# Inner pairs of four duos in one unit with x standing, in place of two half-empty units

## The chip, the cores and the metric

The kernel runs on one NeuronCore of a Trainium2 chip. The metric is the device time of one execution in microseconds. Before the change the median of three runs is 1236.45 us (1236.43 to 1236.52).

## The reference

The kernel computes a small recommendation model over a batch of 2048 samples, all in fp32. Each of 40 fields looks up a row of 64 numbers in its own table. For every pair of fields i < j (780 pairs), each with its own 64x64 matrix W, one number is computed: the row of i times W, dotted with the row of j. The 780 numbers and 16 dense inputs of a sample go through three layers.

```python
e = jnp.stack([tbl_0[ids[:, 0]], ..., tbl_39[ids[:, 39]]], axis=1)      # 2048 x 40 x 64
viW = jnp.einsum('bpd,pde->bpe', e[:, i_idx, :], W)                      # 780 pairs
z = jnp.einsum('bpe,bpe->bp', viW, e[:, j_idx, :])
h = jnp.concatenate([z, dense_ctx], axis=1)                              # 796 wide
h = jnp.maximum(h @ W_top1 + b_top1, 0.0)                                # 796 x 512
h = jnp.maximum(h @ W_top2 + b_top2, 0.0)                                # 512 x 256
y = h @ W_top3                                                           # 256 x 1
```

## The kernel before, in words

**Tiles.** The batch is cut into NB = 4 blocks of 512 samples, each of four subs of 128. Two fields form a duo (20 per block), four duos a quad (5 per block). GpSimd gathers a duo's table rows with samples on partitions into `rows` (12 slots, one per duo). TensorE turns a duo with four transposes (`duo`, L908) into PSUM, and ScalarE copies it to `x` (24 slots), where one field's 64 numbers lie on partitions 0 to 63 and the other's on 64 to 127, and 512 samples lie along the columns. For duos 0 to 3 of block 0 nothing is gathered: their rows are looked up by matmuls of small tables, held in SBUF, with tables of zeros and ones that VectorE builds (L1051, `hot`); the result is x directly, and `rows` never holds them.

**Units.** A unit fills two PSUM banks with 128 x 1024 numbers (x times W), and VectorE multiplies them with the other field's numbers in one instruction. There are three kinds:
- F (L940): W stands (it is the operand loaded into the array), x of duo n moves. Two matmuls of 64 x 128 by 512 columns, one in the upper and one in the lower 64 rows of the array. Its result has the numbers of a pair on partitions and samples along columns. It covers four pairs between two duos.
- D: the same instructions for the pairs inside a duo, of two duos at once. Each half of the array computes one pair only, so half of the result's 128 rows belong to no pair. There is one D unit for two duos, 10 per block, counted among the 120 standing units of a block.
- R (L936): x stands, W moves; its result has samples on partitions. It covers 16 pairs for 128 samples; four such units share one chunk of weights. There are 20 chunks, so 80 R units per block. How many of a quad's lower duos are done in this way is MOVED.

**Sums.** The product of an F or D unit (`fprod`, 9 slots) is summed over partitions by TensorE (`sums`, L957): two matmuls with a 128 x 32 operand of ones per unit, four at a time side by side in the array's column strips, into one bank `z_ps`; a group is four units, eight such tiles. The product of an R unit (`rprod_A`, `_V`, `_P`) is summed along its columns, by ScalarE in 16 parts (L1145), by VectorE in one reduce (L1094), or by GpSimd in six halving adds (L865, L870); the sums land in `zb` (5 slots), which TensorE turns with four transposes per chunk of 128 columns (`turn_z`, L974).

**Layers.** Layer 1 has seven chunks of K (four from `z_ps`, three from `zb`) and four output tiles (L988), then layers 2 (L998) and 3 (L1007). Those of a block run as single steps between the units of the next block. The last block's run at the end with nothing beside them.

**Order.** A planner in the file (class Plan) walks through the work with a cost for each step and writes out the instruction order of every engine before the kernel is built. U_SLOTS = 3 units may be in flight between TensorE and VectorE. R units are spread evenly among the F units (`due`). Turning a duo, a sum group or an MLP step is put in preferably where the planner sees TensorE waiting; LEAD says how many duos ahead of need it may turn, MLP_GAP and MLP_PACE how many units apart MLP steps are, ROWS_LEAD how many duos ahead the gathers must be before GpSimd takes sums. The planner also chooses which engine sums an R unit (`owner_of`): ScalarE if it has room, else GpSimd, else VectorE.

Of the kernel before, what the change touches and what calls it, by code (L numbers as in the profile page):

```python
# [42 lines left out]
MOVED = [0, 3, 4, 6, 7]  # L44
# [5 lines left out]
WF_SLOTS, WR_SLOTS = 4, 2  # L50
# [37 lines left out]
NF, NR = len(STANDING), len(MOVING)  # L88
NC = len(CHUNKS_R)
GROUPS = NF // GROUP  # L90
# [5 lines left out]
R_PAIRS = NC * FOLD  # L96
# [6 lines left out]
DENSE_CHUNK, DENSE_ROW = (ZF - 1, 96) if Z_LAST <= 48 else (ZK - 1, R_PAIRS % P)  # L103
assert Z_LAST <= 48 or 0 < DENSE_ROW <= P - DENSE
# [9 lines left out]
def z_strips(k):  # L114
    return 3 if k == ZF - 1 == DENSE_CHUNK else 4


W1_COLS, W2_COLS = ZK * H1, M1 * H2
assert NF % GROUP == 0 and Z_TILES % (2 * GROUP) == 0
# [6 lines left out]
def z_place(t):  # L126

    k, r = divmod(t, Z_TILES)
    strips = z_strips(k)
    return k, r % strips, 2 * (r // strips)  # L130


def tile_pairs(f, half):

    kind, n, k = STANDING[f]
    if kind == "D":
        m = DUOS - 1 - (n - 1 if half == 0 else n)
        pair = (2 * m, 2 * m + 1)
        return (None, pair) if half == 0 else (pair, None)
    i, j = 2 * (DUOS - 1 - n) + half, 2 * (DUOS - 1 - k)  # L140
    return (i, j), (i, j + 1)
# [7 lines left out]

def lay_standing(w):
    out = np.zeros((NF // HALF, P, HALF, P), np.float32)
    for f, (kind, _, _) in enumerate(STANDING):
        for half in range(2):
            for par, pair in enumerate(tile_pairs(f, half)):
                if pair is not None:
                    one = w[pair_index(*pair)]
                    out[f // HALF, half * DIM:(half + 1) * DIM, f % HALF, par * DIM:(par + 1) * DIM] = (  # L160
                        one.T if kind == "D" and half == 1 else one)
    return out.reshape(NF // HALF, P, HALF * P)
# [10 lines left out]

def lay_mlp(w1, b1, w2, b2, w3):
    lay1 = np.zeros((P, ZK, H1), np.float32)
    for t in range(NT):
        k, strip, r = z_place(t)
        for par, pair in enumerate(tile_pairs(t // 2, t % 2)):
            if pair is not None:
                lay1[32 * strip + r + par, k] = w1[pair_index(*pair)]  # L180
    for c in range(NC):
        for a in range(FOLD):
            row = FOLD * c + a
            lay1[row % P, ZF + row // P] = w1[pair_index(*moving_pair(c, a // 8, a % 8))]
    n_pairs = FIELDS * (FIELDS - 1) // 2
# [19 lines left out]
T_HOT, T_BUILD, T_TABLE, T_TABLES = 0.423, 0.35, 6.0, 1.6  # L205

LEAD, LEAST, ROWS_LEAD = 4, 1, 4
# [3 lines left out]
MLP_GAP, MLP_PACE = 6, 14  # L211

AHEAD, BEHIND = 2, 10

# [8 lines left out]
class Plan:  # L223


    def __init__(self):
# [25 lines left out]
    def rows_free(self, v):  # L252
# [4 lines left out]
        if old < HOT:  # L257
            return self.builds_at[-1] if len(self.builds_at) == len(HOT_STEPS) else None
# [88 lines left out]
    def take(self, u, ready):  # L347

        _, kind, n, _ = self.units[u]
        if kind == "R":  # L350
            b = self.units[u][0]
            ready = max(ready, *(self.arrived[v] for v in range(DUOS * b + 4 * CHUNKS_R[n][0], DUOS * b + 4 * CHUNKS_R[n][0] + 4)))
# [4 lines left out]
        if kind == "R":  # L357
# [63 lines left out]
    def do_duo(self):  # L421
# [34 lines left out]

    def do_sums(self, b, g):
# [5 lines left out]
        for h in range(2):  # L463
            t = max(t, self.prod_at[self.f_units[first + HALF * (h + 1) - 1]]) + T_SUMS / 2
# [9 lines left out]
    def step_ready(self, ev):  # L474
# [36 lines left out]
    def do_unit(self, unit):  # L511
        u = len(self.units)
        v = DUOS * unit[0] + (CHUNKS_R[unit[2]][1] if unit[1] == "R" else unit[2])
# [7 lines left out]
        self.pe_t, self.mode = t + T_UNIT, "main"  # L521
# [3 lines left out]
    def run(self):  # L525
        self.done = {}
        sums, mlp, last_step = [], [], -MLP_PACE
        for b in range(NB):
            base, f, r = DUOS * b, 0, 0
            mlp += [("zr", b, c) for c in range(ZR)]  # L530
            while f < NF or r < NR:
# [8 lines left out]
                ready_r = r < NR and base + CHUNKS_R[MOVING[r][1]][1] < turned and (  # L540
                    self.arrived.get(base + 4 * CHUNKS_R[MOVING[r][1]][0] + 3, 9e9) <= self.pe_t + 1)
# [12 lines left out]
                if unit:  # L554
                    v = base + (CHUNKS_R[unit[2]][1] if unit[1] == "R" else unit[2])
# [3 lines left out]
                if sums:  # L559
                    last = NF * sums[0][0] + GROUP * sums[0][1] + GROUP - 1  # L560
# [6 lines left out]
                must_sum = sums and unit and unit[1] != "R" and (  # L567
# [4 lines left out]
                if must_step:  # L572
                    what = "step"
                elif must_sum:
# [655 lines left out]
```

## Time and profile before

| | |
|---|---|
| median of 3 runs | 1236.45 us |
| profiled execution | 1235.92 us, its span 1234.1 us |
| TensorE (PE) busy | 1216.8 us, 99% |
| VectorE (DVE) busy | 1004.4 us, 81% |
| ScalarE (ACT) busy | 954.5 us, 77% |
| GpSimd (POOL) busy | 781.1 us, 63% |
| granted TensorE clock | 1.00 of full speed in all stretches |

The profile is of one execution. PE rows are matmuls and PEld rows are loads of the standing operand, which run beside matmuls. A fp32 matmul of the program shows as two loads and two matmuls. The ends of matmuls are modelled, so a PE that is busy isn't always at its peak, and times from start to start say more than durations. VectorE instructions overlap by about 0.09 us in the same way. L957 is line 957 of the kernel before.

### The profile page before, as it was taken

The page shows a single profiled execution, that of the slowest core. Times are in us where ns is not written, and L with a number is a line of the kernel's source. Part 1 is how long each engine was busy: PE and PEld are TensorE (multiplying, and loading weights), DVE is VectorE, ACT ScalarE, POOL GpSimd, SP SyncE. Part 2 cuts the span into 40 slices and gives each one's busy share as a digit, 9 for nine tenths or more (in the row PEclk, how much of TensorE's full clock was granted, in tenths as well). Part 3 has the DMA queues.
Part 4 walks back from the last instruction along what each step waited for, and adds up shares of the span by engine and source line. Part 5 has one row for each costly group of instructions (what it writes and reads, how often), then busy time and mean ns, then how long its engine had stood idle before and what let it go on. Part 6 is the DMA issues. An engine that isn't in the chain of part 4 may idle for free.

```text
span 1234.1 us, 23139 instructions
## 1 busy us (share of the span) xinstructions
PE 1216.8 (99%) x5912; PEld 445.5 (36%) x5912; DVE 1004.4 (81%) x916; ACT 954.5 (77%) x7377; POOL 781.1 (63%) x1038
## 2 busy tenths in 40 slices
PE   7999999999999999999999999999999999999999
PEld 3333333333333333333333333333333333333333
DVE  7898999998787788898767868889787876788850
ACT  2174878998383889999688899999778899999841
POOL 8888883686655577777656666778766566423320
DMA  7332222222222222222222222222222222111100
GB/s 200 110 86 66 67 75 58 70 70 65 64 64 60 50 76 64 65 75 63 70 58 59 68 57 66 67 74 65 61 71 65 62 59 61 54 49 57 43 10 1
DMA packets 68477, 81.00 MB, mean 66 GB/s; under 512 B 15308, under 2 KB 46028, under 8 KB 68216
## 3 DMA queue, kind: packets, MB, share of 16 engines
q1 hardware_dynamic: 48752, 59.42, 16.1%
q0 software_dynamic: 19456, 19.96, 9.0%
q8 instruction: 48, 0.79, 0.3%
q14 instruction: 85, 0.70, 0.2%
q10 hardware_dynamic: 136, 0.14, 0.0%
HBM read 79.45 MB, written 0.01 MB: 64 GB/s over the span
## 4 chain that ended last, share of the span: by engine, by line
PE 95%; DVE 3%; issue 1%; ACT 1%; DMA 0%; SPq 0%; DVEq 0%
PE u_ps L940 35%; PE u_ps L936 23%; PE z_ps L957 19%; PE turn_ps L988 7%; PE turn_ps L908 3%; PE turn_ps L901 2%; PE turn_ps L998 2%; PE u_ps L988 2%; DVE acts L1051 1%; DVE fprod L1088 1%; PE u_ps L998 1%; PE turn_ps L974 1%; DVE rprod_A L1075 0%; DMA rows<-in_first_ids 0%; PE turn_ps L1007 0%
## 5 line engine op out<-in xcount | busy, mean ns | idle before, releaser
L1145 ACT ACTIVATE rprod_A<-rprod_A 128x64 f32<-128x64 f32 x3616 | 866.3, 242 | 105.2 <-DVE rprod_A L1075 102.7
L845 POOL DMA_INDIRECT rows<-in_tbl,ids_all x608 | 575.3, 946 | 274.1 <-issue 112.6
L1145 ACT ACTIVATION_READ_ACCUMULATOR rprod_A<-rprod_A 128x1 f32 x3616 | 680.3, 188 | 0.0
L1088 DVE TENSOR_TENSOR fprod<-u_ps,x 128x1024 f32<-128x1024 f32 x480 | 567.4, 1219 | 50.6 <-PE u_ps L940 50.0
L940 PE MATMUL u_ps<-x,wf_ring 64*128 64x512 f32 x1920 | 490.1, 607 | 3.6 <-ACT x L1132 1.8
L1075 DVE TENSOR_TENSOR rprod_A<-u_ps,rows 128x1024 f32<-128x1024 f32 x226 | 274.9, 1222 | 131.5 <-PE u_ps L936 131.5
L936 PE MATMUL u_ps<-wr_ring,x 64*128 64x512 f32 x1280 | 347.5, 612 | 0.7 <-DVE rprod_A L1075 0.5
L940 PEld LDWEIGHTS u_ps<-x,wf_ring 64*128 64x128 f32 x1920 | 175.1, 186 | 252.9 <-issue 186.7
L957 PE MATMUL z_ps<-fprod,ones 128*32 128x512 f32 x1920 | 251.9, 598 | 0.0
L865 POOL TENSOR_TENSOR rprod_P<-rprod_P 128x512 f32<-128x512 f32 (+4 forms) x245 | 148.5, 606 | 131.3 <-DVE rprod_P L1075 115.4
L936 PEld LDWEIGHTS u_ps<-wr_ring,x 64*128 64x128 f32 x1280 | 116.7, 186 | 171.2 <-issue 93.7
L957 PEld LDWEIGHTS z_ps<-fprod,ones 128*32 128x32 f32 x1920 | 55.4, 109 | 177.9 <-issue 95.1
L1132 ACT COPY x<-turn_ps 128x512 f32<-128x512 f32 x80 | 45.5, 569 | 86.4 <-PE turn_ps L908 55.4
L988 PE MATMUL turn_ps<-acts,mlp_sb 128*128 128x512 f32 (+2 forms) x182 | 84.1, 607 | 0.9 <-ACT acts L1161 0.9
L1075 DVE TENSOR_TENSOR rprod_P<-u_ps,rows 128x1024 f32<-128x1024 f32 x49 | 59.7, 1219 | 0.0
L1094 DVE TENSOR_REDUCE zb<-rprod_V 128x16 f32<-128x1024 f32 x45 | 54.3, 1221 | 0.3
L1075 DVE TENSOR_TENSOR rprod_V<-u_ps,rows 128x1024 f32<-128x1024 f32 x45 | 54.2, 1223 | 0.0
L908 PEld LDWEIGHTS turn_ps<-ident,rows 128*128 128x128 f32 x304 | 31.8, 140 | 58.3 <-issue 56.0
L988 PEld LDWEIGHTS turn_ps<-acts,mlp_sb 128*128 128x128 f32 (+2 forms) x182 | 32.4, 189 | 51.2 <-issue 49.4
L908 PE MATMUL turn_ps<-ident,rows 128*128 128x128 f32 x304 | 49.9, 287 | 0.0
L854 POOL MEMSET pause<- 128x256 f32 x128 | 46.2, 361 | 0.1
L901 PE MATMUL turn_ps<-acts,mlp_sb 125*64 125x512 f32 x136 | 36.2, 641 | 10.0 <-DMA mlp_sb<-in_tbl 7.1
(37 smaller groups left out, 193.2 us busy)
## 6 DMA issues: line engine op xcount, KB each, us to landing
wf_ring<-in_w_standing SPq DMA_DIRECT2D x240, 128.0 KB
wr_ring<-in_w_moving SPq DMA_DIRECT2D x80, 256.0 KB
rows<-in_tbl,ids_all POOLq DMA_INDIRECT x608
mlp_sb<-in_mlp SPq DMA_DIRECT2D x1, 2308.0 KB, 9.6
mlp_sb<-in_tbl SPq DMA_DIRECT2D x6, 224.0 KB
rows<-in_first_ids SPq DMA_DIRECT2D x4, 256.0 KB, 5.8
rprod_P<-in_first_ids SPq DMA_DIRECT2D x4, 256.0 KB, 8.8
mlp_sb<-in_tbl SPq DMA_DIRECT2D x2, 280.0 KB
```

Source lines behind the costliest of these rows:

```text
L845: nc.gpsimd.indirect_dma_start(rows[:, v % ROW_SLOTS, s, par * DIM:(par + 1) * DIM], None, tables[f], bass.IndirectOffsetOnAxis(ap=ids_all ...
L865: nc.gpsimd.tensor_tensor(of[:, :, 0:width], of[:, :, 0:width], of[:, :, width:2 * width], ALU.add).then_inc(fold_step, 1)
L901: op = pe.matmul(bank[h % 2 * DIM:(h % 2 + 1) * DIM, :], tables_sb[:, at:at + DIM], hot[0:HOT_PARTS, i % HOT_SLOTS, :], start=(c == 0), st ...
L908: op = pe.transpose(bank[:, s * P:(s + 1) * P], rows[:, v % ROW_SLOTS, s, :], ident[:])
L936: op = pe.matmul(u_ps[:, bank + half, :], x[on, x_slot(b, of), k * P:(k + 1) * P], wr_ring[on, c % WR_SLOTS, :], start=True, stop=True)
L940: op = pe.matmul(u_ps[:, bank + half, :], wf_ring[on, c % WF_SLOTS, f % HALF * P:(f % HALF + 1) * P], x[on, x_slot(b, m), :], start=True, ...
L957: op = pe.matmul(z_ps[32 * strip:32 * strip + 32, :], ones[:, 30 - row:62 - row], fprod[:, f % FPROD_SLOTS, t % 2, :], start=(r < strips), ...
L988: op = pe.matmul(bank[:, :], w1_sb[0:n_rows, k, m * P:(m + 1) * P], z_sb[0:n_rows, z_slot(b, k), :], start=(k == 0), stop=(k == ZK - 1))
L1075: nc.vector.tensor_tensor(products_of(u).rearrange("p h (a d) -> p h a d", a=4), u_ps[:, bank:bank + 2, :].rearrange("p h (a d) -> p h a d ...
L1088: nc.vector.tensor_tensor(fprod[:, f % FPROD_SLOTS], u_ps[:, bank:bank + 2, :], other, ALU.mult).then_inc(prods_done, 1)
L1094: nc.vector.tensor_reduce(sums_at(u, 0, FOLD), products_of(u).rearrange("p h (e d) -> p (h e) d", d=DIM), AX.X, ALU.add).then_inc(r_sums[" ...
L1145: op = nc.scalar.activation(of[:, j, :], of[:, j, :], ACT.Copy, accum_out=sums_at(u, j, 1))
```

## The change

- The D units are gone. `STANDING` holds F units alone: 110 per block, 27 groups of four and a last one of two.
- A new kind I stands for the inner pairs of the four duos of a quad, one unit per quad, five per block. x stands and W moves, as in an R unit: for each of two duos per half and each of four subs one matmul with 64 x 128 of x standing and a 64 x 64 W moving, 16 matmuls in all. Its result has samples on partitions (a duo and a sub take 64 columns), and it is summed over d by ScalarE, VectorE or GpSimd, as R units are. Its weights come in a ring of their own (`wi_ring`, 64 KB per load).
- The I unit of a quad comes behind the quad's R units in the order of moving units (85 per block).
- VectorE needs the rows of duos 0 to 3 of block 0 for the I unit of quad 0. They are turned back from x to `rows` by TensorE (`back`, four transposes per duo) and copied by ScalarE.
- MOVED goes from 0, 3, 4, 6, 7 to 0, 3, 4, 5, 8. The sum is the same.
- The dense inputs lie in the last chunk of layer 1, behind the columns of the I units, and no longer in the last `z_ps` chunk.
- The planner's numbers T_BUILD, T_TABLE, LEAD, ROWS_LEAD and MLP_GAP change; T_INNER and BACK are new. GpSimd's pause writes to a slot of `zb` and no longer to a tile of its own.

```diff
-MOVED = [0, 3, 4, 6, 7]
+MOVED = [0, 3, 4, 5, 8]
...
-WF_SLOTS, WR_SLOTS = 4, 2
+WF_SLOTS, WR_SLOTS, WI_SLOTS = 4, 2, 2
...
-def standing_units():
-    out = []
-    for n in range(DUOS):
-        if n % 2:
-            out.append(("D", n, n - 1))
-        out += [("F", n, k) for k in range(MOVED[n // 4], n)]
-    return out
-
-
-STANDING = standing_units()
+STANDING = [("F", n, k) for n in range(DUOS) for k in range(MOVED[n // 4], n)]
 CHUNKS_R = [(q, k) for q in range(QUADS) for k in range(MOVED[q])]
-MOVING = [("R", c, s) for c in range(len(CHUNKS_R)) for s in range(SUBS)]
+MOVING = [unit for q in range(QUADS) for unit in
+          [("R", c, s) for c, (of, _) in enumerate(CHUNKS_R) if of == q for s in range(SUBS)] + [("I", q, 0)]]
...
-GROUPS = NF // GROUP
+GROUPS = -(-NF // GROUP)
...
-R_PAIRS = NC * FOLD
+R_PAIRS = NC * FOLD + DUOS
...
-DENSE_CHUNK, DENSE_ROW = (ZF - 1, 96) if Z_LAST <= 48 else (ZK - 1, R_PAIRS % P)
-assert Z_LAST <= 48 or 0 < DENSE_ROW <= P - DENSE
+STRIPS = 4
+
+DENSE_CHUNK, DENSE_ROW = ZK - 1, R_PAIRS % P
+assert 0 < DENSE_ROW <= P - DENSE
...
+def lay_inner(w):
+
+    out = np.zeros((QUADS, P, 2, DIM), np.float32)
+    for q in range(QUADS):
+        for a in range(4):
+            one = w[pair_index(*inner_pair(4 * q + a))]
+            half = a // 2
+            out[q, half * DIM:(half + 1) * DIM, a % 2] = one.T if half else one
+    return out.reshape(QUADS, P, 2 * DIM)
...
-T_HOT, T_BUILD, T_TABLE, T_TABLES = 0.423, 0.35, 6.0, 1.6
-
-LEAD, LEAST, ROWS_LEAD = 4, 1, 4
+T_INNER = 1.75
+T_HOT, T_BUILD, T_TABLE, T_TABLES = 0.423, 0.535, 8.5, 1.6
+
+LEAD, LEAST, ROWS_LEAD = 8, 1, 5
 
 STALL, GAP = 0.05, -0.3
 
-MLP_GAP, MLP_PACE = 6, 14
+MLP_GAP, MLP_PACE = 8, 14
 
 AHEAD, BEHIND = 2, 10
+
+BACK = 2
...
+                elif back and turned >= HOT and (stall > STALL or u >= BACK) and self.bank_at <= soon:
+                    what = "back"
...
+    def do_back(self, n):
+
+        self.order.append(("back", 0, n))
+        self.pe_t = max(self.pe_t + self.turn_to("turn"), self.bank_at, self.copied[n]) + T_DUO
+        self.mode = "turn"
+        self.arrived[n] = self.bank_at = self.do_act(("copy", ("back", 0, n)), self.pe_t + LAG_PE, T_COPY)
...
-        pause = sb("pause", [P, 2 * P])
...
+        pause = zb[:, ZB_SLOTS - 1, 0:2, :].rearrange("p s c -> p (s c)")
...
+        def sum_at(u, j):
+
+            _, kind, _, s = ALL[u]
+            k, column = zb_chunk(u)
+            if kind == "I":
+                s, j = j % SUBS, j // SUBS
+            return zb[:, k % ZB_SLOTS, s, column + j:column + j + 1]
...
-                if ROW_SLOTS <= v < ROW_SLOTS + HOT and part == 0:
-
-                    pool.wait_ge(hot_built, len(HOT_STEPS))
-                    pool.sem_inc(rows_free, 1)
-                elif v >= ROW_SLOTS and part == 0:
+                if v >= ROW_SLOTS and part == 0:
                     old_b, old_n = divmod(v - ROW_SLOTS, DUOS)
...
+                if kind == "I":
+                    for a, s in [(a, s) for a in range(2) for s in range(SUBS)]:
+                        to = slice((SUBS * a + s) * DIM, (SUBS * a + s + 1) * DIM)
+                        for half, on in enumerate(halves):
+                            op = pe.matmul(u_ps[:, bank + half, to],
+                                           x[on, x_slot(b, of[2 * half + a]), s * P:(s + 1) * P],
+                                           wi_ring[on, I_AT[u] % WI_SLOTS, a * DIM:(a + 1) * DIM],
+                                           start=True, stop=True)
...
+            def back(n):
+
+                ev = ("back", 0, n)
+                bank = bank_for(ev, TURN_AT[ev])
+                pe.wait_ge(turn_read, TURN_AT["duo", 0, n] + 1)
+                for s in range(SUBS):
+                    op = pe.transpose(bank[:, s * P:(s + 1) * P], x[:, x_slot(0, n), s * P:(s + 1) * P], ident[:])
+                op.then_inc(turned, 1)
...
             def sums(b, g):
-                for t in range(2 * GROUP * g, 2 * GROUP * (g + 1)):
+                for t in range(2 * GROUP * g, 2 * min(GROUP * (g + 1), NF)):
...
-                if kind == "R":
+                if kind != "F":
                     e = OWNER[u]
                     i = SUM_AT[u]
                     if i >= RPROD_SLOTS[e]:
 
                         dve.wait_ge(r_sums[e], i - RPROD_SLOTS[e] + 1)
-                    first = (DUOS * b + 4 * CHUNKS_R[n][0]) % ROW_SLOTS
-                    if (b, CHUNKS_R[n][0]) not in landed:
-                        for slot in range(first, first + 4):
-                            turn = rows_turn(DUOS * b + 4 * CHUNKS_R[n][0])
-                            dve.wait_ge(rows_in[slot], 2 * 16 * SUBS * turn)
-                        landed.add((b, CHUNKS_R[n][0]))
+                    q = quad_of(kind, n)
+                    first = (DUOS * b + 4 * q) % ROW_SLOTS
+                    if (b, q) not in landed:
+                        if DUOS * b + 4 * q < HOT:
+                            dve.wait_ge(turn_read, TURN_AT["back", 0, HOT - 1] + 1)
+                        else:
+                            for slot in range(first, first + 4):
+                                dve.wait_ge(rows_in[slot], 2 * 16 * SUBS * rows_turn(DUOS * b + 4 * q))
+                        landed.add((b, q))
+                    if kind == "I":
+
+                        at = rows[:, first, 0, DIM:P]
+                        by = bass.AP(at.tensor, at.offset, [at.ap[0], [8 * P - DIM, 2], [P, 2 * SUBS], [1, DIM]])
+                        nc.vector.tensor_tensor(products_of(u).rearrange("p h (a d) -> p h a d", d=DIM),
+                                                u_ps[:, bank:bank + 2, :].rearrange("p h (a d) -> p h a d", d=DIM),
+                                                by, ALU.mult).then_inc(prods_done, 1)
+                        return
...
-                if kind == "D":
-                    s0, s1 = x_slot(b, n - 1), x_slot(b, n)
-                    other = x[:, s0:s1 + 1, :]
-                else:
-                    other = x[:, x_slot(b, k):x_slot(b, k) + 1, :].to_broadcast([P, 2, BLOCK])
+                other = x[:, x_slot(b, k):x_slot(b, k) + 1, :].to_broadcast([P, 2, BLOCK])
...
+            def back(n):
+                bank = bank_of(("back", 0, n))
+                nc.scalar.copy(rows[:, n, :, :].rearrange("p s c -> p (s c)"), bank[:, :]).then_inc(turn_read, 1)
```

## Rows read from the trace of the kernel before

**Rows 1.** The page: busy time by engine, and the chain's shares by engine and line.
```profile
PE 1216.8 (99%) x5912; PEld 445.5 (36%) x5912; DVE 1004.4 (81%) x916; ACT 954.5 (77%) x7377; POOL 781.1 (63%) x1038
...
PE 95%; DVE 3%; issue 1%; ACT 1%; DMA 0%; SPq 0%; DVEq 0%
PE u_ps L940 35%; PE u_ps L936 23%; PE z_ps L957 19%; PE turn_ps L988 7%; PE turn_ps L908 3%; PE turn_ps L901 2%; PE turn_ps L998 2%; PE u_ps L988 2%; DVE acts L1051 1%; DVE fprod L1088 1%; PE u_ps L998 1%; PE turn_ps L974 1%; DVE rprod_A L1075 0%; DMA rows<-in_first_ids 0%; PE turn_ps L1007 0%
```

**Rows 2.** The chain in order of time, 640 to 660 us: start, us, what.
```profile
644.62 1.85 PE z_ps L957 x16
646.47 1.92 PE u_ps L940 x8
648.39 0.86 PE u_ps L936 x4
...
650.10 0.59 PE turn_ps L908 x4
```

**Rows 3.** Busy times by stretch: length, PE, PEld, DVE, ACT, POOL, clock, DMA share, GB/s.
```profile
60.00:120.00 60.00, 58.13 (x318) 20.19 (x314) 52.97 (x48) 32.51 (x249) 53.06 (x84) 1.00 0.31 82
120.00:300.00 180.00, 178.51 (x897) 61.28 (x896) 177.28 (x157) 156.07 (x1240) 127.75 (x185) 1.00 0.27 70
300.00:540.00 240.00, 239.91 (x1180) 89.74 (x1180) 197.35 (x173) 179.73 (x1388) 159.91 (x193) 1.00 0.26 64
...
600.00:840.00 240.00, 239.91 (x1182) 89.60 (x1180) 190.19 (x166) 208.99 (x1634) 160.62 (x194) 1.00 0.26 65
```

**Rows 4.** Instructions in order of time, VectorE, 640 to 660 us: start, us, what.
```profile
643.23 1.21 DVE L1075 TENSOR_TENSOR rprod_P<-u_ps,rows 128x1024 f32<-128x1024 f32 x1
644.36 1.21 DVE L1088 TENSOR_TENSOR fprod<-u_ps,x 128x1024 f32<-128x1024 f32 x1
```

**Rows 5.** Instructions in order of time, TensorE, 1156 to 1172 us.
```profile
1159.58 2.77 PE L957 MATMUL z_ps<-fprod,ones 128*32 128x512 f32 x16
1162.28 1.13 PE L936 MATMUL u_ps<-wr_ring,x 64*128 64x512 f32 x4
...
1169.28 2.77 PE L957 MATMUL z_ps<-fprod,ones 128*32 128x512 f32 x16
```

**Rows 6.** The page's groups: count, busy and mean ns, idle before.
```profile
L1145 ACT ACTIVATE rprod_A<-rprod_A 128x64 f32<-128x64 f32 x3616 | 866.3, 242 | 105.2 <-DVE rprod_A L1075 102.7
L845 POOL DMA_INDIRECT rows<-in_tbl,ids_all x608 | 575.3, 946 | 274.1 <-issue 112.6
...
L940 PE MATMUL u_ps<-x,wf_ring 64*128 64x512 f32 x1920 | 490.1, 607 | 3.6 <-ACT x L1132 1.8
...
L1094 DVE TENSOR_REDUCE zb<-rprod_V 128x16 f32<-128x1024 f32 x45 | 54.3, 1221 | 0.3
...
L854 POOL MEMSET pause<- 128x256 f32 x128 | 46.2, 361 | 0.1
```

**Rows 7.** Order of time, weight loads (PEld), then matmuls, 608 to 609.7 us.
```profile
608.54 0.36 PEld L974 LDWEIGHTS turn_ps<-ident,zb 128*64 128x64 f32 x4 [0.76 <-issue]
609.09 0.30 PEld L940 LDWEIGHTS u_ps<-x,wf_ring 64*128 64x128 f32 x4 [0.20 <-issue]
...
608.54 0.63 PE L974 MATMUL turn_ps<-ident,zb 128*64 128x128 f32 x4
609.10 1.13 PE L940 MATMUL u_ps<-x,wf_ring 64*128 64x512 f32 x4
```

**Rows 8.** Order of time, VectorE and weight loads, 1157 to 1159.5 us.
```profile
1157.16 1.21 DVE L1075 TENSOR_TENSOR rprod_P<-u_ps,rows 128x1024 f32<-128x1024 f32 x1
...
1158.49 0.33 PEld L940 LDWEIGHTS u_ps<-x,wf_ring 64*128 64x128 f32 x4 [0.89 <-issue]
```

**Rows 9.** Order of time, VectorE, 0 to 75 us.
```profile
8.81 18.82 DVE L1051 TENSOR_SCALAR acts<-rows,row_of 125x512 f32<-125x512 f32 x35 [2.06 <-ACT rows L1120]
...
49.12 6.88 DVE L1088 TENSOR_TENSOR fprod<-u_ps,x 128x1024 f32<-128x1024 f32 x6 [2.23 <-PE u_ps L940]
57.70 1.23 DVE L1088 TENSOR_TENSOR fprod<-u_ps,x 128x1024 f32<-128x1024 f32 x1 [1.70 <-PE u_ps L940]
```

More of the change, by code:

```diff
@@ L147, in moving_pair, with inner_pair, quad_of, stands @@
     return 2 * (DUOS - 1 - 4 * q - e // 2) + e % 2, 2 * (DUOS - 1 - k) + half
+def inner_pair(n):
+    return 2 * (DUOS - 1 - n), 2 * (DUOS - 1 - n) + 1
+def quad_of(kind, n):
+    return n if kind == "I" else CHUNKS_R[n][0]
+def stands(kind, n):
+    return list(range(4 * n, 4 * n + 4)) if kind == "I" else [CHUNKS_R[n][1]]
+def first_column(kind, n):
+    return FOLD * NC + 4 * n if kind == "I" else FOLD * n
+def units_until(c):
+    return 1 + max(r for r, (kind, n, _) in enumerate(MOVING) if first_column(kind, n) < P * (c + 1))
 def lay_standing(w):
     out = np.zeros((NF // HALF, P, HALF, P), np.float32)
-    for f, (kind, _, _) in enumerate(STANDING):
+    for f in range(NF):
         for half in range(2):
             for par, pair in enumerate(tile_pairs(f, half)):
[L158 to L161, printed above, removed]
+                out[f // HALF, half * DIM:(half + 1) * DIM, f % HALF,
+                    par * DIM:(par + 1) * DIM] = w[pair_index(*pair)]
     return out.reshape(NF // HALF, P, HALF * P)
@@ L184, in lay_mlp @@
             lay1[row % P, ZF + row // P] = w1[pair_index(*moving_pair(c, a // 8, a % 8))]
+    for n in range(DUOS):
+        row = first_column("I", n // 4) + n % 4
+        lay1[row % P, ZF + row // P] = w1[pair_index(*inner_pair(n))]
     n_pairs = FIELDS * (FIELDS - 1) // 2
@@ L349, in take @@
         _, kind, n, _ = self.units[u]
-        if kind == "R":
-            b = self.units[u][0]
-            ready = max(ready, *(self.arrived[v] for v in range(DUOS * b + 4 * CHUNKS_R[n][0], DUOS * b + 4 * CHUNKS_R[n][0] + 4)))
+        if kind != "F":
+            first = DUOS * self.units[u][0] + 4 * quad_of(kind, n)
+            ready = max(ready, *(self.arrived[v] for v in range(first, first + 4)))
             self.owner_of(u, ready)
@@ L462, in do_sums @@
             t = max(t, self.z_at[-1])
-        for h in range(2):
-            t = max(t, self.prod_at[self.f_units[first + HALF * (h + 1) - 1]]) + T_SUMS / 2
+        for last in range(first + HALF - 1, NF * b + min(GROUP * (g + 1), NF), HALF):
+            t = max(t, self.prod_at[self.f_units[last]]) + T_SUMS / 2
             self.half_at.append(t + LAG_PE)
@@ L526, in run @@
         self.done = {}
-        sums, mlp, last_step = [], [], -MLP_PACE
+        sums, mlp, last_step, back = [], [], -MLP_PACE, list(range(HOT))
         for b in range(NB):
@@ L566, in run @@
                 soon = self.pe_t + max(stall, 0.3)
-                must_sum = sums and unit and unit[1] != "R" and (
+                must_sum = sums and unit and unit[1] == "F" and (
                     len(self.f_units) + 1 - FPROD_SLOTS >= NF * sums[0][0] + GROUP * sums[0][1])
@@ L719, in dlrm_tower @@
         wr_in = [sem(f"wr_in{s}") for s in range(WR_SLOTS)]
+        wi_in = [sem(f"wi_in{s}") for s in range(WI_SLOTS)]
         rows_free = sem("rows_free")
@@ L801, in _ @@
                 load_table(h)
+            for i in range(WI_SLOTS):
+                load_inner(i)
             for c in range(min(WR_SLOTS, NC)):
@@ L937, in unit @@
                                        wr_ring[on, c % WR_SLOTS, :], start=True, stop=True)
-                    else:
-                        m = n - 1 if kind == "D" and half == 0 else n
+                else:
+                    for half, on in enumerate(halves):
                         op = pe.matmul(u_ps[:, bank + half, :],
                                        wf_ring[on, c % WF_SLOTS, f % HALF * P:(f % HALF + 1) * P],
-                                       x[on, x_slot(b, m), :], start=True, stop=True)
+                                       x[on, x_slot(b, n), :], start=True, stop=True)
```

170 lines of the change are left out of this document (90 added, 80 removed).

## Prediction

> **What bounds the kernel now.** I read the page's busy shares and its chain of waits first. TensorE is busy for 99% of the span, VectorE for 81%, ScalarE for 77%, and 95% of the chain that ended last lies on TensorE [rows 1]. The reader is to see there that the unit matmuls hold 35% + 23% of the span and the column sums (z_ps) 19%. A busy TensorE can still be a waiting one, since the ends of matmuls are modelled, so next comes the chain in order of time [rows 2]: in a stretch without stalls a unit of four matmuls takes 0.86 us, a sum group of sixteen takes 1.85 us, and the unit that follows a change of shape takes 1.06 instead of 0.86 (the two behind the sum group 1.92 together). A sum group thus costs 1.85 + 0.20 = 2.05 us, of which 16 x 0.43 / 4 = 1.72 us is streaming and 0.33 the two changes of shape. A turned duo costs 0.59 + 0.20 = 0.79 us.
>
> Then I read the busy times by stage [rows 3]. From 300 to 540 us VectorE is busy for 197 of 240 us and a product starts every 1.13 us at the closest [rows 4], so TensorE sets the pace. From 120 to 300 us VectorE is busy for 177.3 of 180 us: there VectorE sets the pace, because block 0 has no MLP steps of an earlier block for TensorE to do between units, and ScalarE, at 156 of 180 us, leaves 19 whole sums to VectorE. The third kind is the end of a block. In the last block two sum groups start 9.70 us apart with seven units between them (most of their rows are left out) [rows 5]. TensorE's own work for that is 7 x 0.86 + 2.05 = 8.07 us and VectorE's 7 x 1.13 = 7.9: neither is full. The group lasts 2.77 us instead of 1.92, because it waits for the product of the unit just before it, and VectorE then waits for the next unit. I call the last 60 us of each block such a stretch.
>
> **The counts.** Per block the change takes 10 D units and puts 5 I units. MOVED keeps its sum (20 chunks, so 80 R units), and its F units stay 6 + 10 + 22 + 34 + 38 = 110. Units go from 200 to 195 per block, products of VectorE with them; column sums from 120 units (30 groups) to 110 (27 groups and a half one); units to be summed over d by ScalarE, GpSimd or VectorE from 80 to 85. W_top1 stays at seven chunks (220 tiles still need 4, 340 columns still need 3), and four zr transposes per chunk stay, so the MLP steps cost the same, and so does the tail after 1196 us. Moving the dense rows to the last chunk takes away nothing on TensorE.
>
> **TensorE, part by part, all four blocks.**
> Sums: 30 x 2.05 = 61.5 us per block before; after, 27 x 2.05 + (0.86 + 0.33) = 56.5. That removes 5.0 us per block, 19.8 in all.
> D units: 40 x 0.86 = 34.4 us removed.
> I units: 20 are added, each of 16 small fp32 matmuls. An fp32 matmul shows as two loads and two matmuls in the trace (1920 for 480 units of two halves, [rows 6]), so one I unit is 32 loads of 64x128 and 32 matmuls of 64 columns, in two row groups. A 512-column matmul streams for 0.43 us, so 64 columns stream for 0.054. The loads are the cost. Four loads of an F unit are over in 0.30 us while its four matmuls run to 1.13 [rows 7]: the halves load side by side, each half's second load is done behind its first matmul, and with 0.19 us for one load the second starts 0.11 after the first. Transposes agree: four 64-column loads take 0.36 us in all, and their four matmuls 0.63 with 0.27 for one, a step near 0.11. So I take 16 steps of 0.109 = 1.74 us per I unit, 34.9 in all: the exchange of 40 D for 20 I costs +0.5 us. The bound below is streaming alone, 16 x 0.054 = 0.86 us (-17.7 in all), which the 0.30 for two loads rules out. The bound above is the densest mix of instructions that the trace sustains, 32 in the 1.85 us of a sum group, 0.058 each: 64 x 0.058 = 3.7 us (+39). It is far off: after a wait that ended with the product at 1158.37, four loads have started and ended by 1158.82 [rows 8]; with 0.19 for the last, at least six instructions were issued in some 0.15 us, 0.025 each, and 64 x 0.025 = 1.6 is below 1.74.
> On one point a rule of the Trainium skill speaks against this. In "TensorE: Matmul & The Clock Gate", Part 3 (the mechanism), it says that a weight load overlaps a running matmul only when the row group differs. By that rule each I step would be load plus stream, 0.163 us, and a unit 2.61. The trace disagrees: in the 0.30 us row both halves' second loads end while both row groups are streaming.
> Back turns: four transposes of duos 0 to 3 to their rows, since the table path of block 0 never gathers them and the I unit of quad 0 needs them: 4 x 0.79 = 3.2 us after 48 us, with four more ScalarE copies, for which ScalarE has room (32.5 of 60 us busy, [rows 3]).
> TensorE's work thus changes by -19.8 + 0.5 + 3.2 = -16.1 us.
>
> **VectorE and the summing engines.** VectorE loses 20 products: 20 x 1.13 = 22.6 us. The I product reads 64-wide pieces of rows from PSUM partners in another order; products of both present patterns take 1.22 us [rows 4], I take the same, and the bounds I can give are 1.13 and twice that, the second costing nothing where TensorE leads (43 of 240 us idle). The 20 new sums cost 16 x 0.24 = 3.84 us on ScalarE (3616 parts for 226 sums), 1.13 on VectorE (a reduce is as long as a product, 45 of them before) [rows 6]. ScalarE has about 280 us idle in the whole, but is at 209 of 240 us in block 2, so some of them go to VectorE. Under TensorE's lead that is free.
>
> **What lies on the path.**
> Block 0 is VectorE's: -5 x 1.13 = -5.6 for products; the back turns delay units at 50 us, where VectorE is idle for want of them [rows 9], so their 3.2 us are paid in full; of five new sums I give half to VectorE, +2.8 (ends 0 and +5.6). Sum +0.4 us, ends -2.4 and +3.2. TensorE's 5 us are lost here: VectorE is late next.
> Blocks 1 to 3: TensorE's -5.0 + 0.1 = -4.9 us per block are gained whole in the leading 240 of 310 us (-3.8). In the last 60 to 70 us both engines lose about 1.1 us of work (5 x 1.13 x 70 / 310 is 1.3 for VectorE); the wait between them eats some of it: -0.8, ends 0 and -1.3. Sum -4.6 each, -13.8.
> The planner may now turn duos 8 ahead instead of 4 (LEAD) and has truer costs for the table builds (0.535 where 35 of them take 18.82 us, [rows 9]). Four duos more, turned while TensorE waits at a block's end, are worth 4 x 0.79 = 3.2 us per block and 9.5 for three; twelve row slots and the gathers stand against it. I take -1, ends 0 and -9.5. GpSimd's gathers for duos 12 to 15 now wait for the I product of quad 0 instead of for the table builds; it comes near 60 us, and 64 gathers stand before them at 0.95 us and a pause of 0.36 each [rows 6], 84 us, so this costs nothing. The loads of weights get fewer bytes (220 for 240 of 128 KB, and 20 of 64 KB), on a DMA share of 0.27 [rows 3].
> Sum: +0.4 - 13.8 - 1.0 = -14.4 us. The profiled execution took 1235.92 us (span 1234.1 and 1.8 around it); after, 1221.5. The median of the runs is 0.5 above the profiled one: 1222 us.
>
> **The rivals.**
> 1. The loads don't hide (the rule above, as a mechanism of this kernel: 0.109 + 0.054 per step). 20 x (2.61 - 1.74) = +17.4 us, so 1239: slower. For it: the trace has no 64-column matmul behind a load. Against: the 0.30 us row. It decides from 2.46 us per I unit on, where 20 x 0.72 has used up the 14.4.
> 2. Instructions arrive at 0.058 us each: 3.7 us per I unit, +39, 1261 us: slower by far. Against: [rows 8].
> 3. VectorE's lead spreads: nearly all new sums fall to it, the block ends lengthen, and blocks 1 to 3 give 2.5 us each instead of 4.6, block 0 loses 3: -5 us, 1231. For it: ScalarE is nearly full in blocks 2 and 3 and in block 0. Against: 43 to 50 us of VectorE idle per 240.
> 4. The stalls at block ends are filled as well (LEAD, fewer products): -9.5 more and block 0 at its good end, -26, 1210 us. For it: some 6 us of waiting per block end. Against: an I unit now holds a quad's row slots longer.
>
> **How the numbers follow.** Forecast 0.69 (own range 1215 to 1229), rival 1 0.07, rival 2 0.03, rival 3 0.13, rival 4 0.08. A measurement of this kernel tells 0.2% (2.5 us) from no change. Faster takes the forecast but 0.02, rival 3 but 0.03, and rival 4: 0.85. Same takes those 0.05 and 0.01 of rival 1, which lies at its edge: 0.06. Slower is the rest of rivals 1 and 2: 0.09. The range to hold 8 in 10 is 1209 to 1233: it takes in both ends of the block ends, the end of LEAD, rival 3 and most of rival 4, and leaves out rivals 1 and 2.
>
> **What would show it.** In the trace after: 1760 unit matmuls of the F line and 640 of a new line, 1760 of z_ps; an I unit's 32 matmuls from first to last start in 1.70 us, (2.6: rival 1; over 3: rival 2), and the next unit right behind. Chain share of z_ps near 18%. VectorE's products 780, its reduces between 50 and 60; more than 60 speaks for rival 3. The stretch 120 to 300 us still full on VectorE, and block 0 ending no earlier than before, within 3 us; each later block some 4.6 us shorter. The forecast is wrong if I units take over 2 us, if block 0 becomes 5 us shorter or longer, or if TensorE stalls appear at the quad changes, where an I unit waits for rows or for a zb slot.

## The result, and the profile after

The changed kernel takes 1197.39 us (median of 4 runs, 1196.95 to 1198.54) where the kernel before takes 1236.44: a ratio of 0.9686, 95% interval 0.9669 to 0.9702. That is 39 us, and 14.4 were forecast. The time lies far below the range of 1209 to 1233.

The page of the changed kernel, busy times and the chain, answers to [rows 1]:

```profile
PE 1177.7 (99%) x6248; PEld 457.7 (38%) x6248; DVE 1003.0 (84%) x915; ACT 966.7 (81%) x7477; POOL 774.4 (65%) x1026
...
PE 89%; DVE 5%; issue 4%; ACT 1%; POOL 1%; DMA 0%; SPq 0%; DVEq 0%; ACTq 0%; POOLq 0%
PE u_ps L1007 30%; PE u_ps L1003 23%; PE z_ps L1032 16%; PE turn_ps L1063 7%; PE turn_ps L965 3%; PE u_ps L997 3%; PE turn_ps L958 2%; DVE fprod L1172 2%; PE turn_ps L1073 2%; PE u_ps L1063 2%; DVE acts L1128 1%; DVE zb L1180 1%; DVE rprod_A L1163 1%; PE u_ps L1073 1%; ACT rprod_A L1234 1%
```

L1007 is the F unit, L1003 the R unit, L997 the I unit, L1032 the sums. TensorE is 39.1 us less busy (1216.8 to 1177.7), as much as the whole gain. VectorE is as busy as before: 20 products fewer, 19 reduces more. The sums' share of the chain fell from 19% of 1234 us to 16% of 1195, where I had expected near 18%: some 43 us, where I had counted 19.8. Shares are rounded; added up from the trace, from the first matmul of each sum group to the next other matmul, the sums hold TensorE for 243.2 us before and 204.3 after, 38.9 less. That is the row that says where the prediction lost its size.

The step that was disputed, the I unit, is in TensorE's timeline of the changed kernel, weight loads first, then matmuls:

```profile
646.59 1.86 PEld L997 LDWEIGHTS u_ps<-wi_ring,x 64*128 64x128 f32 x32 [0.17 <-issue]
...
646.59 2.00 PE L997 MATMUL u_ps<-wi_ring,x 64*128 64x64 f32 x32
648.52 1.92 PE L1032 MATMUL z_ps<-fprod,ones 128*32 128x512 f32 x16
```

Thirty-two loads end 1.86 us after the first starts, so 16 loads in a row group follow each other (1.86 - 0.19) / 15 = 0.111 us apart. The matmuls hide behind them: forecast 0.109 and 1.74 us.

From the first matmul of each block (worked out from the trace by counting unit matmuls) come the lengths of the stages, in us:

| | to block 1 | block 1 | block 2 | block 3 and tail | span |
|---|---|---|---|---|---|
| before | 315.3 | 293.8 | 293.1 | 331.9 | 1234.1 |
| after | 307.1 | 284.9 | 283.4 | 319.8 | 1195.2 |
| forecast change | +0.4 | -4.6 | -4.6 | -4.6 | (-1 more for the planner) |
| measured change | -8.2 | -8.9 | -9.7 | -12.1 | -38.9 |

### The profile page after: what moved, and what is told of

It is laid out like the page before. It is cut to its first block, busy times and chain, and to the rows that moved or that the text cites. A ratio compares the mean times of both kernels' runs of the same rounds, so it can differ in the third digit from the quotient of the medians.

```text
span 1195.2 us, 23954 instructions
## 1 busy us (share of the span) xinstructions
PE 1177.7 (99%) x6248; PEld 457.7 (38%) x6248; DVE 1003.0 (84%) x915; ACT 966.7 (81%) x7477; POOL 774.4 (65%) x1026
## 4 chain that ended last, share of the span: by engine, by line
PE 89%; DVE 5%; issue 4%; ACT 1%; POOL 1%; DMA 0%; SPq 0%; DVEq 0%; ACTq 0%; POOLq 0%
PE u_ps L1007 30%; PE u_ps L1003 23%; PE z_ps L1032 16%; PE turn_ps L1063 7%; PE turn_ps L965 3%; PE u_ps L997 3%; PE turn_ps L958 2%; DVE fprod L1172 2%; PE turn_ps L1073 2%; PE u_ps L1063 2%; DVE acts L1128 1%; DVE zb L1180 1%; DVE rprod_A L1163 1%; PE u_ps L1073 1%; ACT rprod_A L1234 1%
## 5 line engine op out<-in xcount | busy, mean ns | idle before, releaser
L1172 DVE TENSOR_TENSOR fprod<-u_ps,x 128x1024 f32<-128x1024 f32 x440 | 524.0, 1222 | 32.1 <-PE u_ps L1007 31.9
L1007 PE MATMUL u_ps<-x,wf_ring 64*128 64x512 f32 x1760 | 444.9, 604 | 2.3 <-DVE fprod L1172 0.7
L1163 DVE TENSOR_TENSOR rprod_A<-u_ps,rows 128x1024 f32<-128x1024 f32 x213 | 260.5, 1224 | 98.0 <-PE u_ps L1003 97.8
L1003 PE MATMUL u_ps<-wr_ring,x 64*128 64x512 f32 x1280 | 338.7, 614 | 0.1
L1007 PEld LDWEIGHTS u_ps<-x,wf_ring 64*128 64x128 f32 x1760 | 158.6, 186 | 219.4 <-issue 163.9
L1032 PE MATMUL z_ps<-fprod,ones 128*32 128x512 f32 x1760 | 212.4, 598 | 0.0
L1003 PEld LDWEIGHTS u_ps<-wr_ring,x 64*128 64x128 f32 x1280 | 110.2, 185 | 172.7 <-issue 92.8
L1032 PEld LDWEIGHTS z_ps<-fprod,ones 128*32 128x32 f32 x1760 | 45.9, 109 | 147.1 <-issue 73.2
L1063 PE MATMUL turn_ps<-acts,mlp_sb 128*128 128x512 f32 (+1 forms) x182 | 81.6, 599 | 0.9 <-ACT acts L1249 0.9
L1180 DVE TENSOR_REDUCE zb<-rprod_V 128x16 f32<-128x1024 f32 x64 | 77.5, 1225 | 1.2
L1163 DVE TENSOR_TENSOR rprod_V<-u_ps,rows 128x1024 f32<-128x1024 f32 x62 | 75.4, 1226 | 0.1
L1063 PEld LDWEIGHTS turn_ps<-acts,mlp_sb 128*128 128x128 f32 (+1 forms) x182 | 33.5, 190 | 47.6 <-issue 46.5
L908 POOL MEMSET zb<- 128x256 f32 x128 | 46.0, 360 | 0.1
```

What stands on the lines that cost most here:

```text
L1003: op = pe.matmul(u_ps[:, bank + half, :], x[on, x_slot(b, of[0]), k * P:(k + 1) * P], wr_ring[on, c % WR_SLOTS, :], start=True, stop=True)
L1007: op = pe.matmul(u_ps[:, bank + half, :], wf_ring[on, c % WF_SLOTS, f % HALF * P:(f % HALF + 1) * P], x[on, x_slot(b, n), :], start=True, ...
L1032: op = pe.matmul(z_ps[32 * strip:32 * strip + 32, :], ones[:, 30 - row:62 - row], fprod[:, f % FPROD_SLOTS, t % 2, :], start=(r < STRIPS), ...
L1063: op = pe.matmul(bank[:, :], w1_sb[0:n_rows, k, m * P:(m + 1) * P], z_sb[0:n_rows, z_slot(b, k), :], start=(k == 0), stop=(k == ZK - 1))
L1163: nc.vector.tensor_tensor(products_of(u).rearrange("p h (a d) -> p h a d", a=4), u_ps[:, bank:bank + 2, :].rearrange("p h (a d) -> p h a d ...
L1172: nc.vector.tensor_tensor(fprod[:, f % FPROD_SLOTS], u_ps[:, bank:bank + 2, :], other, ALU.mult).then_inc(prods_done, 1)
```

## The experiments

**Whose doing is it: the planner's numbers or the exchange of units?** A first accounting, by the times between matmul starts, gave 18 us of TensorE work and 20 us of what I took for stalls. Four kernels were to part the two.

The changed kernel with the old look-ahead (e1):

```diff
-LEAD, LEAST, ROWS_LEAD = 8, 1, 5
+LEAD, LEAST, ROWS_LEAD = 4, 1, 4
```

> The changed kernel with LEAD 4 and ROWS_LEAD 4 as before (8 and 5 in the change). After the change the median is 1197.4 us, 39 us below before; accounting the matmul starts of both traces, 18.3 us of it are TensorE work (predicted 16.1) and 19.9 us are TensorE stalls that are gone (44.8 to 24.9), which I had not forecast. Theory T (the planner's numbers took the stalls away): about half of the 20 us come back, 1207 to 1217. Theory X (the exchange of D for I units took them away, since VectorE has fewer products per block and an I unit gives it 1.74 us for a 1.13 us product): no more than 3 us come back, 1197 to 1200.

Measured: 1207.75 us, ratio 0.9772 (0.9755 to 0.9788). Half of the 20 us seemed to come back, as theory T had it.

The kernel before with the new numbers, D units kept (e2):

```diff
-T_HOT, T_BUILD, T_TABLE, T_TABLES = 0.423, 0.35, 6.0, 1.6
+T_HOT, T_BUILD, T_TABLE, T_TABLES = 0.423, 0.535, 8.5, 1.6
-LEAD, LEAST, ROWS_LEAD = 4, 1, 4
+LEAD, LEAST, ROWS_LEAD = 8, 1, 5
-MLP_GAP, MLP_PACE = 6, 14
+MLP_GAP, MLP_PACE = 8, 14
```

> The kernel before with all planner numbers of the change (T_BUILD 0.535, T_TABLE 8.5, LEAD 8, ROWS_LEAD 5, MLP_GAP 8), its D units kept. Theory T: 1236.4 - 20 = 1216, within 5. Theory X: no change, 1234 to 1239, and its matmul starts still show over 40 us of stalls.

Measured: 1233.94 us, ratio 0.9981 (0.9971 to 0.9991). Theory T falls: the numbers alone are worth 2.3 us, and theory X's time (1234 at least) is met to 0.06 us.

The first line of that edit alone (e3):

> The kernel before with T_BUILD 0.535 and T_TABLE 8.5 alone: the planner then knows that the 68 table builds of VectorE take 12.6 us longer than it thought (68 x 0.185). Theory T1 (the planner of before ran some 12 us ahead of the chip through the whole kernel, and its waits stood in the wrong places): 1220 to 1228, most of what e2 shows. Theory T2 (only LEAD counts): 1235 to 1238. Theory X: 1235 to 1238.

Measured: 1246.41 us, ratio 1.0077 (1.0060 to 1.0094). Truer costs made the plan worse by 10 us. None of the theories had that.

The kernel before with the new MOVED (e4):

```diff
-MOVED = [0, 3, 4, 6, 7]
+MOVED = [0, 3, 4, 5, 8]
```

> The kernel before with MOVED 0, 3, 4, 5, 8 of the change, everything else as before: same counts of F, D and R units. Theories T and X: no change beyond 3 us, 1233 to 1239. If it is 5 us or more faster, the shift of one chunk from quad 3 to quad 4 is part of the cause.

Measured: 1241.95 us, ratio 1.0047 (1.0030 to 1.0064): 5.5 us slower, so not a part of the cause.

**Where the sums' time went.** Neither theory was left whole. I then listed how long each sum group holds TensorE, from its first matmul to the next other one. Before, 25 of 120 groups take over 2.3 us; in e2, e3 and e4 it is 24 to 26; in the changed kernel and in e1 none (their last full group and the half one run straight into each other and are not counted). The weight loads of such a group before, from the very stretch of [rows 5]:

```profile
1159.58 0.15 PEld L957 LDWEIGHTS z_ps<-fprod,ones 128*32 128x32 f32 x6 [0.76 <-DVE fprod L1088]
1160.03 0.12 PEld L957 LDWEIGHTS z_ps<-fprod,ones 128*32 128x32 f32 x3 [0.30 <-issue]
1160.46 0.12 PEld L957 LDWEIGHTS z_ps<-fprod,ones 128*32 128x32 f32 x3 [0.31 <-issue]
1160.89 0.12 PEld L957 LDWEIGHTS z_ps<-fprod,ones 128*32 128x32 f32 x2 [0.31 <-DVE rprod_A L1075]
1161.32 0.12 PEld L957 LDWEIGHTS z_ps<-fprod,ones 128*32 128x32 f32 x2 [0.31 <-issue]
```

The loads come in threes, one set every 0.43 us. The one gap that the profile puts down to a product is as short as the others (0.31 us), so the group is not waiting for anything in between: it runs in three column strips. The code says so too: `z_strips` gives 3 for the last z_ps chunk as long as the dense rows lie there (the change has `STRIPS = 4` in its place). Eight tiles of two matmuls over three strips are six waves, over four strips four. Two waves of 0.43 us are 0.86 per group, six groups per block lie in that chunk, 24 x 0.86 = 20.6 us. The 25th long group, at 112 us in block 0, is of another kind: its loads come in eights and then a gap of 0.67 us is ended by a product. To test it, one edit leaves the D units and the planner's order as they were (e5):

```diff
-DENSE_CHUNK, DENSE_ROW = (ZF - 1, 96) if Z_LAST <= 48 else (ZK - 1, R_PAIRS % P)
-assert Z_LAST <= 48 or 0 < DENSE_ROW <= P - DENSE
+DENSE_CHUNK, DENSE_ROW = ZK - 1, R_PAIRS % P
+assert 0 < DENSE_ROW <= P - DENSE
```

> The kernel before with one edit: the dense rows lie in the last zb chunk (DENSE_CHUNK = ZK - 1), so that the last z_ps chunk uses four column strips instead of three. The D units and the planner's order stay as they were, instruction by instruction. Theory S (strips): in the trace before, 25 of 120 sum groups take over 2.3 us, all near block ends, and none in the changed kernel or in e1; six groups per block belong to the last z_ps chunk, whose eight tiles in three strips need two waves of 0.43 us more. 24 x 0.86 = 20.6 us go: 1215 to 1217. Theory P (my reading in the prediction: the groups are long because they wait for a product): no change, 1235 to 1237.

Measured: 1215.76 us, ratio 0.9832 (0.9816 to 0.9849), 20.6 us less. The same stretch of TensorE's timeline in e5, loads, then matmuls, against [rows 5]:

```profile
1144.32 0.16 PEld L957 LDWEIGHTS z_ps<-fprod,ones 128*32 128x32 f32 x8 [0.76 <-DVE fprod L1088]
1144.78 0.13 PEld L957 LDWEIGHTS z_ps<-fprod,ones 128*32 128x32 f32 x4 [0.30 <-issue]
1145.21 0.13 PEld L957 LDWEIGHTS z_ps<-fprod,ones 128*32 128x32 f32 x4 [0.30 <-issue]
...
1144.32 1.92 PE L957 MATMUL z_ps<-fprod,ones 128*32 128x512 f32 x16
...
1153.18 1.92 PE L957 MATMUL z_ps<-fprod,ones 128*32 128x512 f32 x16
```

Loads come in fours, the group is down from 2.77 to 1.92 us, and the period from 9.70 to 8.86. The loads of both groups are released by the same product (`DVE fprod L1088`), so that product was never what made the group long. The edit also changes the shape of layer 1's matmuls (112 and 64 rows become 128 and 80). That isn't where the time went: the sum groups hold TensorE for 223.6 us in e5, 19.6 less than before, and the span is 20.2 shorter. The group at 112 us still takes 2.65 us.

The reverse, three strips put back into the changed kernel, order unchanged (e6):

```diff
+def z_strips(k):
+    return 3 if k == ZF - 1 else 4
...
-    return k, r % STRIPS, 2 * (r // STRIPS)
+    strips = z_strips(k)
+    return k, r % strips, 2 * (r // strips)
...
-                                   start=(r < STRIPS), stop=(r >= tiles - STRIPS))
+                                   start=(r < z_strips(k)), stop=(r >= tiles - z_strips(k)))
```

> The changed kernel with three strips in the last z_ps chunk, its order unchanged. Three full groups and a half one per block lie there: theory S expects 12 x 0.86 + 4 x 0.43 to 0.86 = 12 to 14 us more, 1209 to 1212, and at least 12 sum groups over 2.3 us. Theory P expects 1197 to 1199.

Measured: 1208.78 us, ratio 0.9779 (0.9762 to 0.9795), 11.4 us more than the changed kernel and 0.6 below the forecast of 12. Eleven full groups take 2.70 us, and three of the four half groups 1.83 us instead of 1.00. The twelfth full group and the last half one run into each other and take 3.56 us together; in the changed kernel they take 3.32, with waiting in it, so that little was left to lose there. A group that took 1.92 us takes this again (TensorE, e6):

```profile
585.57 2.77 PE L1037 MATMUL z_ps<-fprod,ones 128*32 128x512 f32 x16
```

**What the rest is worth.** The dense move together with the planner's numbers of e2, D units kept (e7):

> The kernel before with the dense rows moved and all planner numbers of the change; what then parts it from the changed kernel is D against I units, the back turns and MOVED. If the parts add up (theory A): e2 less 20.6 = 1213, and the exchange is worth 1213 - 1197 = 16 us, near the 18 us of TensorE work. If LEAD 8 needs the four strips to pay (theory B, since e1 showed 10 us for it and e2 only 2 with all numbers), it comes to 1203 to 1208.

Measured: 1215.85 us, ratio 0.9831 (0.9815 to 0.9848). With D units the numbers are worth nothing (e5: 1215.76), so theory B falls. Theory A had 1213, 2.9 less, so the parts don't simply add up either. The exchange at the new numbers is worth 1215.9 - 1197.4 = 18.5 us. By stages e5 has 311.9, 288.7, 288.0 and 325.3 us, e7 306.7, 289.6, 291.2 and 326.7: the numbers gain 5.2 us in block 0 and lose 5.5 behind it. From e7 to the changed kernel block 0 changes by +0.4, the others by -4.7, -7.8 and -6.9. Where e7 loses in block 2, its chain in order of time shows:

```profile
881.80 0.94 POOL rows L845
882.75 0.01 issue
882.76 1.29 POOL rprod_P L865
...
886.16 0.23 POOL zb L870
886.38 0.14 issue
886.52 1.03 PE turn_ps L974 x4
887.55 3.71 PE u_ps L940 x8
```

The last zr step of the block (the transposes that turn a chunk of `zb` for layer 1) waits for a sum on GpSimd, and this stands behind gathers that are paced by TensorE's units. The product to be summed is ready at 877.3 us; the sum starts at 882.76, behind four gathers, of which the first had waited for a unit (VectorE, then GpSimd):

```profile
876.04 1.22 DVE L1075 TENSOR_TENSOR rprod_P<-u_ps,rows 128x1024 f32<-128x1024 f32 x1
...
878.05 0.95 POOL L845 DMA_INDIRECT rows<-in_tbl,ids_all  x1 [10.55 <-PE u_ps L940]
```

MOVED put back in the changed kernel (e8):

> The changed kernel with MOVED 0, 3, 4, 6, 7. e4 put the same exchange in the kernel before at +5.5 us for the new value there. If MOVED is neutral in itself and e4 was only another order of the planner, this lies within 5 us of 1197 on either side; if the new value is worse in itself, it is faster, 1190 to 1193.

Measured: 1198.15 us, ratio 0.9690 (0.9671 to 0.9710), no difference from 0.9686. The value isn't worse in itself here. That the 5.5 us of e4 came from the order that the planner made of it in the kernel before is what remains; no run takes that order apart.

The two look-ahead numbers apart, each alone set back to 4 (e9 and e10):

> The changed kernel with LEAD 4 alone, ROWS_LEAD stays 5. e1 (both as before) lost 10.4 us, all of it at the block boundaries, where the last zr step waits for the last sums of the block: on ScalarE's 3.94 us for the last I unit in block 1, on GpSimd in block 2, with only four duos ahead to fill the time. Theory L (the missing filler is the cause): 1205 to 1209. Theory R (ROWS_LEAD 4 put a sum on GpSimd behind a held gather, and the order changed by it): 1197 to 1201.

> The changed kernel with ROWS_LEAD 4 alone, LEAD stays 8. It gives GpSimd 54 sums instead of 47. Theory L: 1197 to 1200, since six to seven duos are still turned ahead. Theory R: 1203 to 1208, with the block 2 boundary waiting for GpSimd again.

Measured: LEAD 4 alone 1202.26 us, ratio 0.9727 (0.9711 to 0.9744), 4.9 us; ROWS_LEAD 4 alone 1200.75 us, ratio 0.9715 (0.9698 to 0.9731), 3.4 us. Both expectations missed: each number has a part, and with 2 us of interplay they make the 10.4 of e1. In e1, e9 and e10 alike the boundary of block 1 shows the same wait; here e1's chain in order of time:

```profile
585.35 1.96 PE u_ps L997 x32
587.31 0.02 issue
587.33 1.24 DVE rprod_A L1158
...
588.65 3.94 ACT rprod_A L1234 x32
592.59 0.25 issue
592.84 0.61 PE turn_ps L1049 x4
```

The last I unit of the block is summed by ScalarE in 3.94 us, and the zr step, and in TensorE's fixed order all behind it, waits for that. In the changed kernel VectorE has this unit in block 1, and more duos are at hand to fill the time.

That is only a part of the 10.4 us. Five F units run on TensorE during that sum, and its own idle time before the zr step is 0.83 us. The longer wait of e1 is in block 2: 3.81 us for a sum on GpSimd, as in e7, and e9 and e10 don't have it. By stages e1 is 1.8, 4.4 and 4.3 us longer than the changed kernel in block 1, block 2, and block 3 with the tail; what makes the last of these isn't shown.

If the sum at the boundary still counts at LEAD 8, giving the last sums to VectorE should help (e11):

```diff
+LAST_V = 2
...
+        if len(self.r_units) % NR >= NR - LAST_V:
+            self.owner[u] = "V"
-        if self.slot_free("A") <= at and backlog <= A_MOST * T_PART * FOLD / 2:
+        elif self.slot_free("A") <= at and backlog <= A_MOST * T_PART * FOLD / 2:
```

> The changed kernel, with the last two moving units of every block (one R and the I unit of quad 4) given to VectorE for their sums, 1.13 us instead of 3.94 on ScalarE. If the zr step at the boundary is what still stands on the path, the boundaries lose 1 to 2 us each: 1192 to 1196. If other work fills the wait at LEAD 8, or VectorE's own queue takes its place: 1196 to 1200.

Measured: 1198.49 us, ratio 0.9698 (0.9681 to 0.9714): no gain. The zr step no longer waits for ScalarE at any boundary, but VectorE's own queue takes its place, one of the two outcomes that the second half of the expectation named. In block 2 the chain runs over product, reduce and the next unit's product, and TensorE's next unit comes behind that:

```profile
868.73 1.24 DVE rprod_V L1162
...
870.05 0.06 DVE zb L1184
...
871.19 1.23 DVE fprod L1176
872.41 0.14 issue
872.55 1.13 PE u_ps L1011 x4
```

Last, the I unit ahead of the last chunk of its quad's R units (e12; the `MOVING` list alone is changed):

> The changed kernel with the I unit before the last chunk of its quad's R units instead of behind them. The last moving unit of a block is then an R unit, whose sum is as long as an I unit's, so no gain from the sum; TensorE's 1.74 us beside VectorE's 1.13 us then lies in the part where VectorE is late. 1194 to 1200; under 1193 or over 1202 would say that where I units stand matters by itself.

Measured: 1195.51 us, ratio 0.9673 (0.9657 to 0.9689). It is the fastest median here, but its interval overlaps with that of the changed kernel, and 1.9 us aren't shown as a gain.

## Why the prediction was wrong

**The step that failed** is in the last part of "The counts": "Moving the dense rows to the last chunk takes away nothing on TensorE." It takes away 20.6 us (e5), more than all else together. The step before it had prepared the miss: "The group lasts 2.77 us instead of 1.92, because it waits for the product of the unit just before it". I priced all sum groups by the one row of 1.85 us in [rows 2] and explained the longer one away as a wait. The same mispricing is in my 30 x 2.05 = 61.5 us of sums per block: with six groups 0.86 longer it is 66.7. The check was in rows 1: 19% of 1234 us is 234 us in the chain, over 120 groups 1.95 each, where groups of 1.85 would make 222.

Of the wait of 9.70 - 8.07 = 1.63 us that I read in [rows 5], the strips were 0.84, and 0.79 stays in e5 (8.86) as a true wait. (The "some 6 us of waiting per block end" of rival 4 doesn't follow from these rows either: 1.63 in every 9.70 us of the last 60 is 10 us.)

Without the strips, 14.4 us forecast stand against 18.4 measured (e5 to the changed kernel). The strips are thus 20.6 of the 24.6 us that the forecast missed; the other 4 lie in block 0.

**The I unit** was right: 0.111 us per load against 0.109, a chain piece of 1.93 us with the entry's 0.20 in it, where 1.74 + 0.20 was forecast. Rivals 1 and 2, with 2.61 and 3.7 us per unit, are dead by the same row. The Trainium skill ("TensorE: Matmul & The Clock Gate", Part 3, the mechanism) says that a load overlaps only with a matmul of another row group; that is rival 1's 2.61 us, and the trace disagrees.

**The exchange of D for I** was near in TensorE's work: 18.3 us less by the accounting of starts, 16.1 forecast. With the strips taken out (from e5 to the changed kernel) the stages give -4.8, -3.8, -4.6 and -5.5 us; the three later blocks sum to -13.9, and -13.8 was forecast. That these agree so well is in part luck. Between kernels with the same planner's numbers (e7 to the changed kernel) the three blocks give -19.4, and from e5 to e1, with the look-ahead of before, -3.4. How much of the work saved on TensorE reaches the time hangs on the planner's order.

In block 0 the exchange with its back turns costs +0.4 (e7 to the changed kernel), as forecast, where VectorE leads. The block still became 8.2 us shorter, which the prediction had named as a sign of being wrong: -3.4 for the strips, -5.2 for the planner's numbers, +0.4 for the exchange. Stretches of the changed kernel, as in [rows 3]:

```profile
120.00:300.00 180.00, 178.67 (x978) 64.60 (x976) 178.86 (x159) 164.30 (x1300) 132.29 (x190) 1.00 0.28 69
300.00:540.00 240.00, 239.15 (x1280) 94.38 (x1280) 204.27 (x179) 190.84 (x1479) 153.04 (x178) 1.00 0.26 64
```

From 120 to 300 us VectorE is busy for 178.9 of 180 us, with 159 instructions for 157 before: the new sums took the place of the products.

**The planner's numbers** were too small a term. I took -1, ends 0 and -9.5; e7 against e5 shows -5.2 in block 0, given back later with D units and not with I units. In the changed kernel LEAD and ROWS_LEAD alone are worth 10.4 us (e1), beyond the end that I had given. They aren't the gain of block 0, which e1 keeps (306.7 us to block 1). MLP_GAP was never tested alone. Nothing in the rows before could have told their size: e3, where truer times cost 10 us, e4, where another MOVED costs 5.5, and e1 show that a change of order is worth 5 to 10 us, for better or worse.

**Rival 3** had its sign in the counts (64 reduces, over the 60 that I had named) and still didn't come: VectorE has 19 reduces more, one of them in block 0 and 18 in blocks 1 to 3, and these blocks became 8.9 us shorter and more. **Rival 4** had the nearest time (1210), but without the strips. Its look-ahead term of 9.5 us has a counterpart in the 10.4 of e1; the exchange without it gave 8.0 (e5 to e1, which has the other new numbers too), where 13.4 were forecast.

## What to carry to other kernels

An instruction group that sometimes takes 1.85 us and sometimes 2.70 has two prices, and neither is explained until its weight loads have been looked at one by one: loads in threes instead of fours told of an idle column strip, not of a wait. Multiply a price taken from one stretch by its count and hold it against the group's share of the chain before it goes into a sum. And where a change moves something "for room", ask what rule the old place had forced on its neighbours: 16 rows of dense inputs had kept a quarter of the array idle in a fifth of all sum groups.

## What the runs showed of the hardware that I had not expected

A long wait costs twice. In e7 TensorE stands idle from 882.6 to 886.5 us, waiting for the sum on GpSimd. Busy times in stretches of 2 us (PE, PEld, DVE, ACT, POOL, then the granted clock):

```profile
882.00:884.00 2.00, 0.58 (x4) 0.00 (x0) 1.23 (x1) 0.00 (x0) 1.99 (x2) 1.00 0.30 59
884.00:886.00 2.00, 0.00 (x0) 0.00 (x0) 0.00 (x0) 0.00 (x0) 1.69 (x5) 0.97 0.12 43
886.00:888.00 2.00, 1.48 (x6) 1.05 (x8) 0.00 (x0) 0.41 (x1) 1.41 (x4) 0.50 0.03 8
888.00:890.00 2.00, 2.00 (x6) 0.67 (x4) 0.39 (x1) 0.17 (x1) 0.95 (x2) 0.50 0.16 33
890.00:892.00 2.00, 2.00 (x8) 0.76 (x6) 1.52 (x2) 0.00 (x0) 1.24 (x2) 0.50 0.08 16
892.00:894.00 2.00, 2.00 (x12) 0.60 (x12) 1.59 (x2) 0.00 (x0) 0.49 (x1) 0.83 0.32 82
```

The granted clock falls to 0.50 (1.2 GHz of 2.4) while TensorE is idle and stays there for over 6 us after it has work again. The transposes take 1.03 us instead of 0.56 to 0.61 and the next two units 3.71 instead of 1.92, so the wait of 3.9 us costs over 2 us more. e1 has a like wait in block 2, 3.81 us, and there the slow stretch is shorter: 0.89 from 880 to 882 us, when TensorE is back at work, 0.50 to 884, 0.76 to 886, then 1.00. Its two units behind the wait take 3.42 us in the chain.
